# Waiting for POOL's own completion at every third indirect transfer in place of every second, in a two-layer graph network on one core

## The chip, the cores and the metric

The kernel runs on one core of a Trainium2 chip. The time is the device time of one execution in microseconds (us). TensorE is PE, VectorE is DVE, ScalarE is ACT, GpSimd is POOL, SyncE is SP.

## The reference

There are N = 100,000 nodes of 128 float32 features and E = 25,000 edges (`src`, `dst`), sorted by `dst`. Two layers follow each other, each with a residual and a layernorm over the features:

```python
x_col = x[col]                                   # row = src, col = dst
feat = concat([x_col, x[row] - x_col], -1)
messages = relu(feat @ W1 + b1) @ W2 + b2
out = segment_max(messages, col)                 # 0 where a node has no edge
x = layernorm(x + out)                           # layer 0

agg = segment_sum(x[src], dst)
h = relu((x + agg) @ W1 + b1) @ W2 + b2
x = layernorm(x + (x @ Wres + bres) + h)         # layer 1
```

Most nodes are the destination of no edge. For them both layers are dense work on their own row alone; rows that have edges must be computed with their neighbours and replace the dense result.

## The kernel before, in words

**Dense work.** Every row of x goes through as if it had no edges: 196 units of 512 rows, four units a body (`SLOTS`), 49 bodies. SP loads a unit and stores its result, DVE normalizes (`x <- x_in, rs_a` is the scaling of the first layernorm), PE transposes and multiplies, ACT evacuates.

**Edge work.** The edges are cut into `GROUPS` = 49 groups of `ROWS` = 512 edges, each group in `TILES` = 4 tiles of 128. One indirect transfer moves one tile: 128 rows of 128 float32, whose row numbers stand in a column of `idx`. All of them are issued by POOL, in an order written out by hand:

1. `gather_src(g)`: the src rows of group g from x into `edge_rows`, a buffer that holds all edges; 38 of the 49 groups first, with four groups of `gather_dst` after group 24.
2. `gather_dst(g)`: the dst rows into `xd_rows`, four slots of one group each. It waits until PE has transposed the group four before it (`tx_done`). After each fourth group one of the remaining 11 src groups is gathered.
3. After both tables of the first layer's edge results are stored (`tabled`) and all rows in `edge_rows` are scaled (`scaled_done`): the gathers of layer 1 from `x1e_table` into `edge_rows`, 49 groups.
4. The scatters of the 49 groups of results from `edge_rows` into the output. The scatter of group g waits for its result (`res_done`) and for the dense stores that cover its rows, so that it overwrites them; the number of stores is read from `stores_16` by POOL's sequencer (`stores_needed`, L635), for group g + 1 ahead of the last of group g's four scatters. At the end of the edge list that is all of the dense stores.

These are 4 x 196 = 784 indirect transfers, all through `gather` (L586) and `scatter` (L593).

**How the engines weave both.** `walk` gives each engine the same order: a body of dense work; then one dense unit a step beside the search for the place of each src row (`step_s`); then half a dense unit a step beside the edge work of layer 0 (`step_a`); then one dense unit a step beside that of layer 1 (`step_b`); then dense work alone. SP copies each gathered group of `edge_rows` into `xs_rows` (`copy_xs`, `copy_xz`, four slots), two groups ahead. In layer 0, DVE runs one scan a group for the segment maximum (L876); in layer 1 one for the sum (L923), and adds the dst rows (`xsT <- shared, x1eT`, L934).

**The pacing.** A transfer's `then_inc(done, 16)` counts when its data has landed. Apart from it, `pace` gives every second transfer a second semaphore, `s_issued`, that POOL itself raises when it has finished the instruction, and `issued_pair` lets POOL wait for it before it issues anything further. The data may still be under way then. All four kinds of transfer share one counter, and since a group has four tiles, the waits stand behind the second and the fourth tile of each group.

Of the kernel before, what the change touches and what calls it, by code (L numbers as in the profile page):

```python
# [44 lines left out]
def gnn_program(nc, x, src, dst, e_w1, e_b1, e_w2, e_b2, w1, b1, w2, b2, wres, bres, out):  # L45
# [21 lines left out]
    with ctx:  # L67
# [6 lines left out]
        def sem(name):  # L74
            return ctx.enter_context(nc.semaphore(name))
# [121 lines left out]
        s_issued = sem("descriptors_written")  # L197
# [357 lines left out]
        def _(pool):  # L555
# [12 lines left out]
            pool.wait_ge(s_dv, SRC_IDX_STEP)  # L568
            SRC, DST, SCAT, PLACE = range(4)
            issued = [0]  # L570

            def pace(kw):

                issued[0] += 1
                if issued[0] % 2 == 0:
                    kw["engine_sem"] = s_issued

            def issued_pair():
                if issued[0] % 2 == 0:
                    pool.wait_ge(s_issued, issued[0] // 2)  # L580

            def gather(to, table, what, t, done):
                kw = {}
                pace(kw)
                rows, err = (GROUPS * ROWS, False) if what == PLACE else (N, True)
                nc.gpsimd.indirect_dma_start(to, None, table, bass.IndirectOffsetOnAxis(idx[:, what, t:t + 1], 0),  # L586
                                             bounds_check=rows - 1, oob_is_err=err, **kw).then_inc(done, 16)
                issued_pair()

            def scatter(table, frm, t, done):  # L590
                kw = {}
                pace(kw)
                nc.gpsimd.indirect_dma_start(table, bass.IndirectOffsetOnAxis(idx[:, SCAT, t:t + 1], 0), frm, None,  # L593
                                             bounds_check=N - 1, oob_is_err=False, **kw).then_inc(done, 16)
                issued_pair()

            def gather_src(g):
                j, r = divmod(g, SLOTS)
                wait(pool, src_gathered[r], 16 * TILES * j)
                for t in range(TILES):  # L600
                    gather(edge_rows[:, cut(g * TILES + t)], x, SRC, g * TILES + t, src_gathered[r])

            def gather_dst(g):
                j, r = divmod(g, SLOTS)
                wait(pool, dst_gathered[r], 16 * TILES * j)
                wait(pool, tx_done, g - SLOTS + 1)
                for t in range(TILES):
                    gather(xd_rows[:, r, cut(t)], x, DST, g * TILES + t, dst_gathered[r])
# [19 lines left out]
            for g in range(GROUPS):  # L628
                j, r = divmod(g, SLOTS)
                wait(pool, z_gathered[r], 16 * TILES * j)  # L630
                for t in range(TILES):
                    gather(edge_rows[:, cut(g * TILES + t)], x1e_table, PLACE, g * TILES + t, z_gathered[r])
# [7 lines left out]
            for g in range(GROUPS):  # L640
                j, r = divmod(g, SLOTS)
                wait(pool, final[r], 16 * TILES * j)
                pool.wait_ge(res_done, g + 1)
                if g < WHOLE:
                    for k in range(SLOTS):
                        pool.wait_ge(stored[k], count)
                    pool.nop().then_inc(s_turn, 1)
                elif g == WHOLE:
                    for k in range(SLOTS):
                        pool.wait_ge(stored[k], 16 * BODIES)  # L650
                for t in range(TILES):
                    if t == TILES - 1 and g + 1 < WHOLE:
                        count = stores_needed(g + 1)
                    scatter(out, edge_rows[:, cut(g * TILES + t)], g * TILES + t, final[r])
# [817 lines left out]
```

## Time and profile before

| what | us |
|---|---|
| median of 3 runs | 1343.35 |
| lowest, highest | 1338.25, 1344.81 |
| profiled execution, its own time | 1332.02 |
| its span, first to last instruction | 1330.2 |
| mean granted clock of TensorE, share of full speed | 0.952 |

The span is what the profile shows; the profiled execution's own time is 1.8 us longer. It is one of the faster executions. Busy times are those of instructions on an engine; waits, branches and the handing over of DMAs are not counted. An "idle before" of a POOL transfer is the time from the end of the previous POOL instruction to its start, and behind the arrow stands who released it. "issue" means that nothing which the profile shows was waited for. Where the releaser of a POOL transfer is a "DMA" by the name of POOL's own transfers, the wait is the one for `s_issued`. Rows with the name POOLq are of POOL's sequencer, which hands instructions over to POOL's cores.

### The profile page before, as it was taken

How to read it: one execution, taken by the hardware profiler on the slowest of the kernel's cores; microseconds unless marked ns; L12 is line 12 of the kernel's file. 1: busy time of each engine (PE TensorE's matmuls, PEld its weight loads, DVE VectorE, ACT ScalarE, POOL GpSimd, SP SyncE). 2: the span in 40 equal slices, each digit the busy share in tenths (PEclk: the TensorE clock that was granted, in tenths of full speed). 3: DMA queues.
4: the chain of work that ended last, by engine and by line, in shares of the span. 5: the costliest groups of instructions: out<-in, count | busy, mean ns of one | idle time of the engine just before them, and what ended most of it. 6: DMA issues, size and time to landing. Idle time of an engine off the chain costs nothing. (4 is left out here: it accounts for less than half of the span.)

```text
span 1330.2 us, 32137 instructions
## 1 busy us (share of the span) xinstructions
PE 1123.7 (84%) x7512; PEld 853.2 (64%) x7512; DVE 1068.6 (80%) x5491; ACT 799.8 (60%) x2305; POOL 825.8 (62%) x797
## 2 busy tenths in 40 slices
PE   2699999998888878788759999999999999999500
PEld 1577777765555545455448888888887777777400
DVE  6599999989887887898838999999987888888400
ACT  0366666666665656667526666666666777777400
POOL 5666666656666666666256666666665666655654
PEclk9899999999998999999979999999999999999855
DMA  4477777756665667666436565656564556656310
GB/s 111 141 220 214 214 220 212 222 188 195 183 208 180 199 174 210 177 205 196 141 112 191 187 185 186 185 187 187 189 190 140 177 181 190 185 181 200 103 38 28
DMA packets 160366, 233.86 MB, mean 176 GB/s; under 512 B 26815, under 2 KB 69273, under 8 KB 160284
## 3 DMA queue, kind: packets, MB, share of 16 engines
q1 hardware_dynamic: 133612, 193.69, 46.7%
q0 software_dynamic: 25088, 38.81, 11.0%
q10 hardware_dynamic: 1584, 0.53, 0.2%
q14 instruction: 62, 0.51, 0.1%
q8 instruction: 20, 0.33, 0.1%
HBM read 129.48 MB, written 90.12 MB: 165 GB/s over the span
## 5 line engine op out<-in xcount | busy, mean ns | idle before, releaser
L1277 PE MATMUL psY<-wcr,xT 128*128 128x128 f32 x1568 | 305.0, 276 | 0.0
L1276 PE MATMUL psY<-wc,hT 128*128 128x128 f32 x1568 | 304.6, 276 | 0.0
L586 POOL DMA_INDIRECT edge_rows<-x1e_table,idx x196 | 210.8, 1075 | 133.2 <-DMA edge_rows<-x1e_table,idx 77.6
L593 POOL DMA_INDIRECT out<-edge_rows,idx x196 | 202.2, 1031 | 129.5 <-issue 76.4
L586 POOL DMA_INDIRECT edge_rows<-in_x,idx x196 | 206.9, 1056 | 116.0 <-DMA edge_rows<-in_x,idx 67.3
L586 POOL DMA_INDIRECT xd_rows<-in_x,idx x196 | 203.5, 1038 | 115.9 <-DMA xd_rows<-in_x,idx 67.3
L1276 PEld LDWEIGHTS psY<-wc,hT 128*128 128x128 f32 x1568 | 255.8, 193 | 15.0 <-issue 8.3
L1123 ACT ACTIVATE o_rows<-psY,rs_b 128x128 f32<-128x128 f32 x784 | 223.0, 367 | 66.7 <-DVE rs_b L741 66.5
L1277 PEld LDWEIGHTS psY<-wcr,xT 128*128 128x128 f32 x1568 | 239.9, 193 | 0.0
L1287 PE MATMUL psH<-xT,wc 128*128 128x512 f32 x392 | 204.5, 604 | 16.0 <-DVE deltas L787 10.6
L1103 ACT ACTIVATE sd_a<-mv_a,eps_col 128x4 f32<-128x4 f32 x196 | 58.3, 298 | 239.6 <-DVE mv_a L677 239.6
L672 DVE BATCH_NORM_STATS2 bn_b<-psY 128x6 f32<-128x128 f32 x784 | 174.4, 285 | 21.9 <-PE psY L1277 7.9
L691 DVE BATCH_NORM_STATS2 bn_a<-x_in 128x6 f32<-128x128 f32 x784 | 173.1, 271 | 0.3 <-DMA x_in<-in_x 0.3
L1267 PEld LDWEIGHTS psT<-ident,x 128*128 128x128 f32 x784 | 99.5, 143 | 106.2 <-issue 104.9
L1092 ACT ACTIVATE hT<-psH,bias_cols 128x512 f32<-128x512 f32 x196 | 131.0, 669 | 5.0 <-PE psH L1287 5.0
L682 DVE TENSOR_TENSOR x<-x_in,rs_a 128x512 f32<-128x512 f32 x196 | 130.6, 666 | 0.3 <-PE psT L1267 0.3
L1267 PE MATMUL psT<-ident,x 128*128 128x128 f32 x784 | 119.5, 276 | 0.9 <-DVE idx L1055 0.9
L1267 PE MATMUL psE<-ident,xs_rows 128*128 128x128 f32 x392 | 61.8, 281 | 60.8 <-ACT ehT L1161 51.6
L1100 ACT COPY xT<-psT 128x512 f32<-128x512 f32 x196 | 112.5, 574 | 0.5 <-PE psT L1267 0.5
L1267 PEld LDWEIGHTS psE<-ident,xs_rows 128*128 128x128 f32 x392 | 45.9, 143 | 98.2 <-issue 83.0
L923 DVE TENSOR_TENSOR_SCAN shared<-mask,shared,psE 128x512 f32<-128x512 bf16 x48 | 61.4, 1279 | 36.5 <-PE psE L1267 23.5
L1287 PEld LDWEIGHTS psH<-xT,wc 128*128 128x128 f32 x392 | 65.8, 194 | 35.6 <-issue 11.0
(135 smaller groups left out, 2042.6 us busy)
## 6 DMA issues: line engine op xcount, KB each, us to landing
x_in<-in_x SPq DMA_DIRECT2D x196, 256.0 KB
out<-o_rows SPq DMA_DIRECT2D x196, 256.0 KB
xs_rows<-edge_rows SPq DMA_DIRECT2D x98, 256.0 KB, 2.9
xs_rows<-src_dram SPq DMA_DIRECT2D x49, 256.0 KB, 4.3
mask<-mask_dram SPq DMA_DIRECT2D x98, 128.0 KB, 3.6
x1e_table<-shared SPq DMA_DIRECT2D x49, 256.0 KB, 2.8
x1eT_spill<-x1eT SPq DMA_DIRECT2D x49, 256.0 KB
x1eT<-x1eT_spill SPq DMA_DIRECT2D x49, 256.0 KB, 2.8
```

The lines of the kernel that those rows point to most:

```text
L586: nc.gpsimd.indirect_dma_start(to, None, table, bass.IndirectOffsetOnAxis(idx[:, what, t:t + 1], 0), bounds_check=rows - 1, oob_is_err=err ...
L593: nc.gpsimd.indirect_dma_start(table, bass.IndirectOffsetOnAxis(idx[:, SCAT, t:t + 1], 0), frm, None, bounds_check=N - 1, oob_is_err=False ...
L672: last = v.bn_stats(bn[:, t, :], rows[:, cut(t)])
L682: v.tensor_tensor(tiles(to), tiles(rows), rs.unsqueeze(2).broadcast_to([P, TILES, P]), ALU.mult).then_inc(done, 1)
L691: last = v.bn_stats(bn_a[:, k % 2, t, :], x_in[:, k, cut(t)])
L1092: a.activation(hT[:, k % 2, :], psH[:, :], ACT.Relu, bias=bias_cols[:, 2:3]).then_inc(hT_done, 1)
L1100: a.copy(xT[:, k, :], psT[:, :]).then_inc(xT_done, 1)
L1123: last = a.activation(o_rows[:, k, cut(t)], psY[k % 2][:, cut(t)], ACT.Copy, scale=rs_b[:, k, t:t + 1])
L1267: last = t_.transpose(to[:, cut(t)], rows[:, cut(t)], ident[:, :])
L1276: t_.matmul(to[:, cut(t)], h[:, cut(t)], wc2[:, :], start=False, stop=False, skip_group_check=True)
L1277: last = t_.matmul(to[:, cut(t)], xt[:, cut(t)], wcr[:, :], start=False, stop=t == TILES - 1, skip_group_check=True)
L1287: t_.matmul(psH[:, :], wc1[:, :], xT[:, k, :], start=True, stop=True).then_inc(w1_done, 1)
```

## The change

The counter of transfers stays, and a count of the waits is added. The semaphore is given to every third transfer (1, 2, **3**, 4, 5, **6**, ...) in place of every second one, and POOL waits behind it, in gathers and in scatters. The number of waits goes from 392 to 261. Nothing else differs: order, sizes and the other semaphores are the same. Since 3 does not divide the four tiles of a group, the waits now stand behind another tile in each group, in a pattern that repeats after three groups. For the scatters, whose first is transfer number 589, they stand behind the third tile in groups 0, 3, 6, ..., behind the second in groups 1, 4, ..., and behind the first and the fourth in groups 2, 5, ...

```diff
             issued = [0]
-
-            def pace(kw):
+            pauses = [0]
+            GATHERS_A_BURST, SCATTERS_A_BURST = 3, 3
+
+            def pace(kw, burst):
 
                 issued[0] += 1
-                if issued[0] % 2 == 0:
+                if issued[0] % burst == 0:
                     kw["engine_sem"] = s_issued
-
-            def issued_pair():
-                if issued[0] % 2 == 0:
-                    pool.wait_ge(s_issued, issued[0] // 2)
+                    pauses[0] += 1
+
+            def issued_burst(burst):
+                if issued[0] % burst == 0:
+                    pool.wait_ge(s_issued, pauses[0])
 
             def gather(to, table, what, t, done):
                 kw = {}
-                pace(kw)
+                pace(kw, GATHERS_A_BURST)
                 rows, err = (GROUPS * ROWS, False) if what == PLACE else (N, True)
                 nc.gpsimd.indirect_dma_start(to, None, table, bass.IndirectOffsetOnAxis(idx[:, what, t:t + 1], 0),
                                              bounds_check=rows - 1, oob_is_err=err, **kw).then_inc(done, 16)
-                issued_pair()
+                issued_burst(GATHERS_A_BURST)
 
             def scatter(table, frm, t, done):
                 kw = {}
-                pace(kw)
+                pace(kw, SCATTERS_A_BURST)
                 nc.gpsimd.indirect_dma_start(table, bass.IndirectOffsetOnAxis(idx[:, SCAT, t:t + 1], 0), frm, None,
                                              bounds_check=N - 1, oob_is_err=False, **kw).then_inc(done, 16)
-                issued_pair()
+                issued_burst(SCATTERS_A_BURST)
```

## Rows read from the trace of the kernel before

**Rows 1.** The page, POOL's busy time and the share of its DMA queue.
```profile
PE 1123.7 (84%) x7512; PEld 853.2 (64%) x7512; DVE 1068.6 (80%) x5491; ACT 799.8 (60%) x2305; POOL 825.8 (62%) x797
...
q0 software_dynamic: 25088, 38.81, 11.0%
```
**Rows 2.** Windows by stage: width, then busy us of each engine, granted clock, DMA share, GB/s.
```profile
60.00:281.00 221.00, 221.00 (x1928) 173.33 (x1927) 217.88 (x1142) 139.01 (x401) 143.31 (x137) 1.00 0.73 212
286.00:645.40 359.40, 296.98 (x1554) 195.48 (x1553) 302.85 (x1367) 229.67 (x603) 234.32 (x224) 0.98 0.64 191
668.20:989.40 321.20, 307.05 (x2098) 253.49 (x2097) 270.48 (x1356) 203.36 (x632) 210.74 (x196) 0.97 0.57 180
...
1251.30:1321.00 69.70, 0.00 (x0) 0.00 (x0) 0.18 (x1) 1.37 (x5) 43.15 (x44) 0.52 0.14 45
```
**Rows 3.** Waits of POOL: us in total, times, longest.
```profile
POOL edge_rows L586 <- issue: 65.0, 199, 2.1
```
**Rows 4.** Timeline of POOL, one pair's end and the next one's start: start, us, what, idle before.
```profile
205.42 1.01 POOL L586 DMA_INDIRECT edge_rows<-in_x,idx  x1 [0.30 <-issue]
207.24 1.01 POOL L586 DMA_INDIRECT edge_rows<-in_x,idx  x1 [0.81 <-DMA edge_rows<-in_x,idx]
```
**Rows 5.** The instructions of L586 and L293 on POOL's sequencer, 206.2 to 208.4 us.
```profile
L586 POOLq MOVE  x2: 29/29/29, 206.5 to 207.0; - x2
...
L293 POOLq EVENT_SEMAPHORE  x1: 17/17/17, 207.6 to 207.6; - x1
```
**Rows 6.** Timeline of POOL at its two real waits.
```profile
286.01 1.34 POOL L586 DMA_INDIRECT xd_rows<-in_x,idx  x1 [5.60 <-PE psE L1267]
...
644.37 1.01 POOL L586 DMA_INDIRECT xd_rows<-in_x,idx  x1 [0.30 <-issue]
668.18 1.00 POOL L586 DMA_INDIRECT edge_rows<-x1e_table,idx  x1 [22.80 <-DMA x1e_table<-shared]
```
**Rows 7.** Waits of PE, 300 to 640 us.
```profile
PE psE L1267 <- ACT ehT L1161: 47.5, 42, 2.0
```
**Rows 8.** Timeline of DVE, two scans of layer 0.
```profile
646.35 1.28 DVE L876 TENSOR_TENSOR_SCAN shared<-mask,shared,psE 128x512 f32<-128x512 bf16 x1 [0.43 <-PE psE L1381]
...
653.62 1.27 DVE L876 TENSOR_TENSOR_SCAN shared<-mask,shared,psE 128x512 f32<-128x512 bf16 x1
```
**Rows 9.** Timeline of DVE, its scalings of dense units.
```profile
752.46 0.66 DVE L682 TENSOR_TENSOR x<-x_in,rs_a 128x512 f32<-128x512 f32 x1
...
759.04 0.66 DVE L682 TENSOR_TENSOR x<-x_in,rs_a 128x512 f32<-128x512 f32 x1
...
1136.54 0.69 DVE L682 TENSOR_TENSOR x<-x_in,rs_a 128x512 f32<-128x512 f32 x1
...
1139.99 0.66 DVE L682 TENSOR_TENSOR x<-x_in,rs_a 128x512 f32<-128x512 f32 x1
```
**Rows 10.** Timeline of POOL: second gathers of two groups, first scatters of two groups.
```profile
752.60 1.38 POOL L586 DMA_INDIRECT edge_rows<-x1e_table,idx  x1 [0.30 <-issue]
...
759.20 1.37 POOL L586 DMA_INDIRECT edge_rows<-x1e_table,idx  x1 [0.30 <-issue]
...
1251.28 0.98 POOL L593 DMA_INDIRECT out<-edge_rows,idx  x1 [1.08 <-issue]
...
1257.71 0.98 POOL L593 DMA_INDIRECT out<-edge_rows,idx  x1 [1.08 <-issue]
```
**Rows 11.** The instructions of L635 and L593 on POOL's sequencer, 1267 to 1268 us.
```profile
L635 POOLq TENSOR_LOAD <-stores x1: 286/286/286, 1267.0 to 1267.0; - x1
...
L593 POOLq MOVE  x1: 29/29/29, 1267.5 to 1267.5; - x1
```
**Rows 12.** Timeline of SP, its last stores (start, and us until the last is handed over).
```profile
1238.82 14.45 SPq L385 DMA_DIRECT2D out<-o_rows  x6
```
**Rows 13.** All of L682's and L934's operations on those tiles: ns min/median/max, first to last start.
```profile
L682 DVE TENSOR_TENSOR x<-x_in,rs_a x196: 651/659/693, 10.0 to 1238.7; 128x512 f32<-128x512 f32 x196
...
L934 DVE TENSOR_TENSOR xsT<-shared,x1eT x49: 658/660/693, 680.1 to 1004.9; 128x512 f32<-128x512 f32 x49
```

## The prediction

> **What bounds the kernel now.** I read the page's first part, then the waits of POOL, then windows over the stages. The reader is to see that the busiest engine, PE, does not set the end: from 1251.3 us on PE has nothing left and DVE 0.18 us, while POOL alone works on for 70 us [rows 1, 2]. POOL is busy for only 62% of the span, yet most of its idle time is short and of its own making: 0.81 us from one transfer's end to the next's start after a transfer that POOL waited for, 0.30 us where it did not wait [rows 4]. A pair costs 1.01 + 0.30 + 1.01 + 0.81 = 3.13 us. POOL makes 784 such transfers in an unbroken chain, with two real waits for others: 5.60 us before the xd_rows gather at 286.01, and 22.80 us before the first gather from x1e_table at 668.18 [rows 6].
>
> These waits cut the run into pieces. Up to 281 us (dense work and the search for places) PE is busy in every microsecond [rows 2], and POOL waits at the end for the first edge step: so this is not POOL's stretch. From 286 to 645 POOL gathers xd_rows and late src rows, and never waits for a consumer. Nor does PE wait for POOL: its waits of 300 to 640 are for ACT alone, as in the one row that holds most of them [rows 7]. One edge step takes 7.3 us (DVE's scan at 646.35 and 653.62) [rows 8]; POOL needs on average 5 transfers for it, 7.8 us, and lives on its lead of four slots. It ends at 645.4 and DVE's scan of the last full step but one runs at 653.62, the transposes of the last group just before it [rows 6, 8]. So this stretch belongs to the engines, but POOL is only some 5 us ahead. From 668.2 to 989.4 POOL gathers 196 tiles, from 991.4 to 1321.0 it scatters 196. PE is busy in nearly all of the gathering stretch, but the gathers go into a buffer that holds all edges, so POOL needn't wait for PE and PE can't be what POOL's end hangs on. The end is: tables stored, 196 gathers, 196 scatters, plus the 9.2 us behind the last scatter (1330.2 - 1321.0).
>
> **A coupling.** In these two stretches about one transfer in four takes nearer 1.4 us than 0.99. At 752.60 a transfer starts while DVE's `x <- x_in, rs_a` runs from 752.46 to 753.12; it takes 1.38 [rows 9, 10]. The excess, 0.39, is what was left of the DVE operation, 0.52, less 0.13 us. So a start that falls in the first 0.54 us of such an operation is held to its end. This locks POOL to the engines: a group of four, of the natural length 4 x 0.99 + 2 x 0.30 + 2 x 0.81 = 6.18 us is stretched to DVE's 6.6 (752.46 and 759.04; POOL's second transfers at 752.60 and 759.20) [rows 9, 10]. Scatters: 4 x 0.98 + 2 x 0.30 + 0.81 + 1.08 = 6.41 natural, as after 1251 us (1251.28 to 1257.71), and about 6.9 beside DVE (two dense units of 3.45: 1136.54 and 1139.99) [rows 9, 10].
>
> **The change, part by part.** It drops 392 - 261 = 131 waits, and moves the rest to every third transfer, so they no longer stand at the group borders.
>
> *The pause.* Its price over a start without one is 0.81 - 0.30 = 0.51 us. The sequencer's rows explain it: after the wait, MOVE at 206.5, the next transfer's MOVE at 207.0 (so some 0.55 us to hand over one transfer), the first transfer's start at 207.24. At 207.6, with the first of the pair still running, the sequencer has handed over the second too and stands at a later instruction [rows 4, 5]. A third would be handed over by 208.2, before the first ends at 208.25. The trace never shows a third in a row. Lower bound of its idle time: 0.30, the second's. Upper: 0.81, what the wait costs, or in the worst case 2.10, the longest idle time that is put down to "issue" [rows 3]. I take 0.30, since the nearest row is a second transfer already waiting in the queue, and the third's handover is hidden in the same way. The Trainium skill (Advanced Engine Details and Errata, Engine Queue Depths) gives GpSimd a queue of 8, by which the third also fits and the sum stays; no row here shows the depth. Were a transfer to fill several places of it, the third would be the slow one of the second rival.
>
> *Up to 668 us.* 392 transfers lose 65 or 66 pauses, 33 us; 14 us of it before 286, where POOL then waits about 20 us in place of 5.6, and 19 us behind, where the wait for the tables grows from 22.8 to about 40. Cover: the edge chain of the engines. Gain of the end: 0. If that cover were gone (POOL slower than now by over 5 us in this stretch), every further microsecond would count.
>
> *Gathers, 668 on.* Three groups (12 transfers): 12 x 0.99 + 8 x 0.30 + 4 x 0.81 = 17.52 us. Holds by DVE: two operations (the other is `xsT <- shared, x1eT`) [rows 13], open for 0.54 us each in 6.6 us, mean hold 0.27: 12 x 1.08/6.6 x 0.27 = 0.5. So 18.0, times 49/3 = 294 us; now 321.2: gain 27. Without a hold 286 (gain 35), with as many as now (0.4 a group) 306 (gain 15). The first tiles come only 0.5 us earlier, so the entry of this stage hardly moves. The consumers: DVE and PE go on at 6.6; results stand ready for the scatters, which start at about 964 and need only those of their own group.
>
> *Scatters.* The read of `stores_16` (TENSOR_LOAD at 1267.0, the next MOVE at 1267.5) lies behind the third scatter, hidden now by a running transfer [rows 11]. In each third group it will stand behind a pause: 0.81 + 0.5 = 1.3. The border (1.08 now, every time) is behind a pause in one group of three. Three groups: 12 x 0.98 + 8 x 0.30 + (0.81 + 0.81 + 1.08 + 1.3) = 18.16, with holds 12 x 0.54/3.45 x 0.27 = 0.5 in five sixths of it 18.6, times 49/3 = 304 us; now 329.6: gain 25. Without holds 297 (gain 32), with today's (0.45 a group) about 317 (gain 12).
>
> *The sum.* 27 + 25 = 52 us; ends: 15 + 12 = 27, and 35 + 32 = 67. A floor cuts the upper one: the last group waits for all dense stores, the last of which is issued at about 1253 [rows 12]. With a 0.8 us start, four scatters in 5.3 us and the 9.2 us behind, and nothing for its landing, no span is under 1268: gain at most 62. The profiled execution has 1332.0 us around its span of 1330.2, so 1332.0 - 52 = 1280. It lies 11.3 us under the median of 1343.35; I take the same 52 off that: 1291. The likeliest case's own range is 1283 to 1316.
>
> *A rule against it.* DVE's operation was never longer than 0.693 us (least 0.651) in 196 times, with a POOL transfer running most of the time [rows 13]: denser starts don't slow DVE. The Trainium skill (SBUF — State Buffer, SBUF: two separate sides) says of the shared port pair that whoever starts first keeps it for the whole instruction; by that, DVE would be held for up to 1 us at a start and the dense work would stretch. The trace shows the hold in one direction only, so nothing is added for it.
>
> **Rivals.** (1) *The third start isn't free but costs near what was saved*, 0.45 to 0.7 us: for it, that nothing in the trace shows three in a row; against it, the sequencer's lead. Break-even: 52 / (2 x 65.3) = 0.40 us above 0.30, so 0.70; where the locking to DVE then fills up the slack, rather 0.55. Time: 1335 to 1350, take 1343.
>
> (2) *Slower: three in a row are one too many.* POOL's core, or the handover behind two waiting ones, makes the third start as late as behind a pause, or later. At 0.81: gathers 12 x 0.99 + 4 x 0.30 + 8 x 0.81 + 0.5 = 20.06, 328 us (+6); scatters 20.6, 338 us (+8); and before 645 a triple costs 4.95 against 4.70 now, 0.085 x 224 = 19 us more, of which 5 are covered: +14. Sum +28: 1371. At 1.08 some +80. It decides from 0.75 us on. For it speaks that POOL has idle times without a releaser of up to 2.1 us [rows 3]; against it, that 199 of them sum to 65.0 us, 0.33 each: nearly all are 0.30.
>
> (3) *Other work gives it back*: POOL's traffic, 11% of the DMA engines' time [rows 1], comes denser, and later loads stretch the dense work. DMA is busy 0.57 to 0.64 in the stretches that count [rows 2], and dense may end 60 us late before it decides. No change, 1340.
>
> **Chances.** Forecast 0.56; rival 1 0.14; rival 2 0.27; rival 3 0.03. Within 0.5% (6.7 us, about what a measurement can tell here) holds most of 1 and 3. Faster 0.58, same 0.13, slower 0.29. For 8 in 10 the range goes from 1281 (0.04 below) up to rival 2's first price, 1372 (0.15 above).
>
> **What the profile after would show.** Right: in bursts of three, idle 0.30, 0.30, 0.81; 261 idle times of 0.81 or more behind a completion; the wait before the first x1e_table gather near 40 us, still at about 668; gathers over by 958 to 964, scatters by 1262 to 1275, with 1.3 us of idle where the read of `stores_16` follows a pause; PE's last matmul still at 1249. Wrong: a third transfer with an idle time or duration of its own over 0.55 us; the first x1e_table gather later than 670; the holds by DVE growing until the group period is again 6.6 and 6.9.

## The result: 14% slower, and the profile after

| | median of the runs | lowest, highest |
|---|---|---|
| before, same chip | 1340.8 us | 1337.31, 1344.81 |
| after | 1534.41 us | 1521.22, 1548.95 |

The ratio is 1.141, with a 95% interval of 1.1304 to 1.1516. The forecast was 1291, its range 1281 to 1372. The profiled execution of after took 1548.95 us, its span is 1547.1; the traces are compared by their spans, 1330.2 and 1547.1. The ratio leaves out the slowest execution of after, which is the profiled one, so it differs a little from the quotient of the medians, and the traces lie 217 us apart where the medians lie 194 apart. Line numbers of after are 3 higher than before's.

First POOL itself. The timeline of POOL after, in the search stretch (columns as in [rows 4]):
```profile
75.95 1.01 POOL L589 DMA_INDIRECT edge_rows<-in_x,idx  x1 [0.30 <-issue]
77.77 1.01 POOL L589 DMA_INDIRECT edge_rows<-in_x,idx  x1 [0.81 <-DMA edge_rows<-in_x,idx]
79.08 1.01 POOL L589 DMA_INDIRECT edge_rows<-in_x,idx  x1 [0.30 <-issue]
80.40 1.01 POOL L589 DMA_INDIRECT edge_rows<-in_x,idx  x1 [0.30 <-issue]
82.23 1.01 POOL L589 DMA_INDIRECT edge_rows<-in_x,idx  x1 [0.81 <-DMA edge_rows<-in_x,idx]
```
This is the forecast to the hundredth: 0.30, 0.30, 0.81, and the third transfer as cheap as the second [rows 4]. In the scatters the read of `stores_16` behind a pause makes 1.37 us of idle time (1094.18), where 1.3 was forecast.

Now the other engines. The same windows as in [rows 2], and then a stretch in which POOL works and the one behind it, in which POOL waits:
```profile
60.00:281.00 221.00, 189.01 (x1354) 133.98 (x1353) 154.94 (x799) 98.56 (x278) 141.62 (x135) 0.92 0.55 161
286.00:645.40 359.40, 296.14 (x1689) 200.80 (x1688) 281.00 (x1320) 210.19 (x556) 176.99 (x172) 0.94 0.58 173
668.20:989.40 321.20, 232.92 (x1248) 171.18 (x1248) 190.87 (x905) 144.00 (x407) 187.21 (x183) 0.88 0.42 129
...
60.00:265.00 205.00, 173.90 (x1229) 122.73 (x1227) 140.68 (x724) 88.23 (x249) 141.01 (x135) 0.92 0.54 161
268.00:350.00 82.00, 81.89 (x721) 64.93 (x720) 80.84 (x432) 53.27 (x154) 0.00 (x0) 1.00 0.59 172
```
In 60 to 281 us PE runs 1354 matmuls where it ran 1928 [rows 2], and DVE and ACT fall with it: 799 for 1142, 278 for 401. The last two rows matter most. While POOL works, PE does 1229 / 205 = 6.0 matmuls per us; once POOL has nothing to do (x0) the same loop goes on at 721 / 82 = 8.8, the pace of before (1928 / 221 = 8.7), with the granted clock at 1.00. So nothing is wrong with PE's own work: it is held while POOL's transfers run.

What the hold looks like, in the timeline of PE after beside the burst of POOL above:
```profile
78.42 0.18 PE L1345 MATMUL psE<-place_w,shared 128*128 128x2 f16 x1
79.13 0.16 PE L1341 MATMUL psE<-place_w,match 128*128 128x2 f16 x1 [0.53 <-issue]
79.16 0.17 PE L1343 MATMUL psE<-place_w,shared 128*128 128x2 f16 x1
79.90 0.16 PE L1345 MATMUL psE<-place_w,shared 128*128 128x2 f16 x1 [0.57 <-issue]
79.92 0.16 PE L1341 MATMUL psE<-place_w,match 128*128 128x2 f16 x1
80.63 0.16 PE L1343 MATMUL psE<-place_w,shared 128*128 128x2 f16 x1 [0.54 <-issue]
```
Matmuls of 0.16 us, most of them with an idle time put down to "issue", come in twos, one two every 0.7 to 0.8 us, from 78.5 us on, in the middle of the burst, until about the time when its pause begins (81.41).

Where the 217 us of span came from, at POOL's landmarks. The timeline of POOL after:
```profile
351.26 1.01 POOL L589 DMA_INDIRECT xd_rows<-in_x,idx  x1 [85.66 <-PE psE L1270]
...
773.25 1.01 POOL L589 DMA_INDIRECT edge_rows<-x1e_table,idx  x1 [37.52 <-DMA x1e_table<-shared]
...
1069.90 1.02 POOL L596 DMA_INDIRECT out<-edge_rows,idx  x1 [1.99 <-issue]
...
1373.14 0.98 POOL L596 DMA_INDIRECT out<-edge_rows,idx  x1 [22.22 <-DMA out<-o_rows]
...
1537.00 0.98 POOL L596 DMA_INDIRECT out<-edge_rows,idx  x1 [0.81 <-DMA out<-edge_rows,idx]
```
- Search stretch: the first xd_rows gather of slot 4 comes at 351.26, not 286.01 [rows 6]: +65.
- Layer 0: the first x1e_table gather at 773.25, not 668.18: 105 late, so another +40.
- Gathers of layer 1: 773.2 to 1067.9, 294.7 us where they took 321.2: -26.5, the forecast's gain of 27, the only place where it is seen.
- Scatters: 1069.9 to 1538.0, 468 us for 330: +138. By the waits of POOL, 147.4 us in 15 waits are for the dense stores ("DMA out<-o_rows"): the dense work has fallen behind, and the scatters that overwrite its rows have to wait for it.

65 + 40 - 26.5 + 138 = 217.

### The profile page after: what moved, and what is told of

Its sections match the earlier page's. It is cut to its first block, busy times and chain, and to the rows that moved or that the text cites. A ratio compares the mean times of both kernels' runs of the same rounds, so it can differ in the third digit from the quotient of the medians.

```text
span 1547.1 us, 32074 instructions
## 1 busy us (share of the span) xinstructions
PE 1240.1 (80%) x7512; PEld 913.8 (59%) x7512; DVE 1072.1 (69%) x5491; ACT 809.8 (52%) x2305; POOL 809.0 (52%) x797
## 3 DMA queue, kind: packets, MB, share of 16 engines
q0 software_dynamic: 25088, 38.81, 9.4%
## 4 chain that ended last, share of the span: by engine, by line
PE 40%; DVE 19%; issue 17%; another core or an unknown queue 12%; ACT 7%; DMA 2%; SPq 1%; DVEq 1%; ACTq 0%; POOL 0%; POOLq 0%
PE psH L1290 7%; PE psY L1280 6%; PE psY L1279 6%; PE psE L1270 4%; PE psT L1270 3%; DVE bn_b L675 3%; DVE bn_a L694 3%; PE psY L1276 2%; DVE shared L926 2%; PE psE L1384 2%; PE psE L1280 2%; PE psE L1279 2%; ACT o_rows L1126 1%; PE psE L1328 1%
## 5 line engine op out<-in xcount | busy, mean ns | idle before, releaser
L596 POOL DMA_INDIRECT out<-edge_rows,idx x196 | 199.9, 1020 | 270.2 <-DMA out<-o_rows 147.4
L1279 PE MATMUL psY<-wc,hT 128*128 128x128 f32 x1568 | 310.9, 279 | 2.7 <-issue 2.0
L1280 PE MATMUL psY<-wcr,xT 128*128 128x128 f32 x1568 | 309.9, 279 | 3.2 <-issue 2.6
L1279 PEld LDWEIGHTS psY<-wc,hT 128*128 128x128 f32 x1568 | 260.5, 196 | 23.0 <-issue 14.5
L589 POOL DMA_INDIRECT edge_rows<-x1e_table,idx x196 | 199.9, 1020 | 132.2 <-issue 66.5
L1280 PEld LDWEIGHTS psY<-wcr,xT 128*128 128x128 f32 x1568 | 243.0, 195 | 6.7 <-issue 5.7
L1290 PE MATMUL psH<-xT,wc 128*128 128x512 f32 x392 | 225.5, 659 | 23.8 <-DVE deltas L790 8.5
L1270 PEld LDWEIGHTS psT<-ident,x 128*128 128x128 f32 x784 | 105.8, 150 | 124.2 <-issue 124.1
L1270 PE MATMUL psT<-ident,x 128*128 128x128 f32 x784 | 127.7, 286 | 6.1 <-issue 5.9
L1270 PE MATMUL psE<-ident,xs_rows 128*128 128x128 f32 x392 | 65.9, 292 | 74.1 <-ACT ehT L1164 47.7
L1290 PEld LDWEIGHTS psH<-xT,wc 128*128 128x128 f32 x392 | 71.4, 212 | 52.4 <-issue 26.4
```

Of the source, the lines that this page charges most:

```text
L1270: last = t_.transpose(to[:, cut(t)], rows[:, cut(t)], ident[:, :])
L1279: t_.matmul(to[:, cut(t)], h[:, cut(t)], wc2[:, :], start=False, stop=False, skip_group_check=True)
L1280: last = t_.matmul(to[:, cut(t)], xt[:, cut(t)], wcr[:, :], start=False, stop=t == TILES - 1, skip_group_check=True)
L1290: t_.matmul(psH[:, :], wc1[:, :], xT[:, k, :], start=True, stop=True).then_inc(w1_done, 1)
```

## The experiments

The same program took very different times on different chips, so each run is read against the kernel before on its own chip: 1361.46 on chip 11 (e1 to e4), 1335.95 on chip 13 (e5 to e8), 1338.56 and 1337.53 on chip 9 (e9 to e12; e17, e18), 1366.45 on chip 8 (e13 to e16). Chips are named by their numbers; the number of the chip on which the result above was taken is not on record.

### Which half, and what about three in a row (chip 11)

**e1, e2: threes in the gathers alone, in the scatters alone.**
```diff
-GATHERS_A_BURST, SCATTERS_A_BURST = 3, 3
+GATHERS_A_BURST, SCATTERS_A_BURST = 3, 2     # e1;  e2: 2, 3
```


> Bursts of three for the gathers only, pairs for the scatters. In the changed kernel PE's instructions came in a trickle (0.7 us apart) wherever POOL ran bursts of three, and at full rate where POOL waited for others. Theory A (two transfers handed over behind a running one hold up the other engines): everything up to the last gather as in the changed kernel (search over at about 350 in place of 281 us, last gather near 1068), then dense work at full rate, 1440 to 1490 us. Theory B (POOL's denser work as such, whatever its grouping): the same here. Theory C (the fault is in the scatters' part or in the dense stores alone): near 1340 us.

> Pairs for the gathers, bursts of three for the scatters only. Theories A and B: up to the last gather as before (989 us), scatters at 6.0 to 6.2 us a group in place of 6.9, but the dense work beside them slower by a quarter; POOL and the dense work end near each other, 1310 to 1350 us. Theory C: most of the 190 us loss is here, over 1450 us.

e1: 1552.06, ratio 1.137 (1.123 to 1.151). e2: 1430.73, ratio 1.048 (1.039 to 1.057). Both halves cost. e1 lies above all that was foreseen for it (1440 to 1490 by theory A), e2 between its two forecasts (1310 to 1350, over 1450). In e2, whose first 588 transfers are the pairs of before, the slot-4 gather came at 325.56 us behind a wait of 47.72, where the trace of before has 286.01 and 5.60: on this chip PE falls behind in the search stretch with pairs too.

**e3: no pause, but never more than one transfer handed over behind the running one; e4: bursts of four.**
```diff
-                if issued[0] % burst == 0:
-                    kw["engine_sem"] = s_issued
-                    pauses[0] += 1
+                kw["engine_sem"] = s_issued
...
-                if issued[0] % burst == 0:
-                    pool.wait_ge(s_issued, pauses[0])
+                if issued[0] > 1:
+                    pool.wait_ge(s_issued, issued[0] - 1)
...
-GATHERS_A_BURST, SCATTERS_A_BURST = 3, 3
+GATHERS_A_BURST, SCATTERS_A_BURST = 4, 4     # e4
```


> Every transfer raises the semaphore, and POOL waits after transfer n only for n - 1: never more than one is handed over behind the running one, and POOL still has no pause (0.30 us between transfers). Theory A (depth of the handover): the engines keep their pace (search over near 281 us, edge step of layer 1 6.6 us), POOL's transfers 1.3 us apart, the time falls to the dense work's floor, 1275 to 1295 us. Theory B (density of POOL's work): at least as slow as the changed kernel, 1530 us or more.

> Bursts of four, waits at the group borders only. Theory A: longer time with two or more waiting, so slower than bursts of three, 1580 to 1700 us. Theory B: rate only 0.04 us a transfer denser, so about 10% more of the same loss, 1540 to 1570 us. Theory D (it was the waits falling inside groups, against the waits for data at the borders): back near 1300 to 1340 us.

e3: 1825.9, ratio 1.339 (1.328 to 1.350). e4: 1737.78, ratio 1.273 (1.261 to 1.285). The windows of the search stretch, one fence for each of e2, e1, e4 and e3 (columns as in [rows 2]):
```profile
60.00:281.00 221.00, 198.88 (x1558) 145.51 (x1577) 179.90 (x924) 113.02 (x322) 140.93 (x136) 0.98 0.61 182
```
```profile
60.00:281.00 221.00, 178.31 (x1258) 125.63 (x1274) 148.23 (x758) 93.19 (x264) 143.47 (x135) 0.91 0.53 154
```
```profile
60.00:281.00 221.00, 148.66 (x798) 97.50 (x807) 94.95 (x487) 60.12 (x170) 140.46 (x135) 0.71 0.38 113
```
```profile
60.00:240.00 180.00, 28.01 (x78) 17.18 (x79) 11.27 (x62) 8.73 (x24) 130.59 (x130) 0.52 0.22 62
245.00:470.00 225.00, 220.54 (x1888) 173.79 (x1913) 217.45 (x1144) 139.09 (x400) 0.00 (x0) 0.98 0.58 169
```
Pairs 1558 matmuls, threes 1258, fours 798 in 221 us on one chip; without a pause 78 in 180 us, 0.43 per us, and 8.4 again as soon as POOL is idle. The granted clock falls with them (0.98, 0.91, 0.71, 0.52, the last near the lower level of 1.2 GHz): it follows PE's standing still and is back at 0.98 when POOL is idle, so it is no cause. e3 has no more transfers handed over ahead than pairs have, and PE stands all the same, so a third one in the queue is not what holds it; e4 puts the pauses back at the group borders and is slower than threes, so their place is not it either. On this chip the loss grows as POOL pauses less. Whether the length of a burst decides or the share of the pauses, these four don't separate. The timeline of PE in e3 shows how slow the stream becomes:
```profile
65.86 0.37 PE L1278 MATMUL psY<-wcr,xT 128*128 128x128 f32 x1 [2.87 <-issue]
68.66 0.37 PE L1277 MATMUL psY<-wc,hT 128*128 128x128 f32 x1 [2.43 <-issue]
71.45 0.37 PE L1277 MATMUL psY<-wc,hT 128*128 128x128 f32 x1 [2.43 <-issue]
74.25 0.37 PE L1278 MATMUL psY<-wcr,xT 128*128 128x128 f32 x1 [2.43 <-issue]
77.06 0.37 PE L1278 MATMUL psY<-wcr,xT 128*128 128x128 f32 x1 [2.43 <-issue]
```
One matmul every 2.80 us, with its weight load between (at 67.26, 70.06, ...), so one instruction every 1.40 us; POOL's transfers start every 1.32 us there, so it isn't one for one. Nor is it only PE's issuing that is late. The timelines of DVE and of ACT in e3:
```profile
100.33 0.89 DVE L673 BATCH_NORM_STATS2 bn_b<-psY 128x6 f32<-128x128 f32 x4 [44.90 <-remote]
```
```profile
117.14 0.59 ACT L1101 COPY xT<-psT 128x512 f32<-128x512 f32 x1 [9.83 <-remote]
```
The matmul at 77.06 is the last that fills this psY, and PE starts nothing more until 119.15. DVE begins on psY 23 us after it. ACT's copy waits in the program only for semaphores that PE raises, and begins 40 us after PE's last instruction and 9.83 us after ACT's own one before. So either what PE reports as done arrives late, or DVE's and ACT's own instructions are held as well; the trace doesn't tell which. POOL is not untouched: from 94.67 to 117.85 us its idle times grow from 0.30 to 0.39 and, four times, to between 1.2 and 1.8. So PE's low count here is in part the engines' waiting in turn for one another: PE starts nothing for 41.7 us from 77.4 on.

### More pause (chip 13)

**e5: a pause behind each transfer** (1, 1). **e6: threes, with a longer pause.**
```diff
                 if issued[0] % burst == 0:
                     pool.wait_ge(s_issued, pauses[0])
+                    rest.append(pool.value_load(row_number[0:1, 0:1], min_val=0, max_val=P))
```


> POOL's own completion waited for after every transfer. Theory 1 (PE gets its instructions and completions through only while POOL pauses; what counts is the share of pauses): 0.81 us of pause for 1.01 us of work, the other engines at full pace: 1739 or a few more PE matmuls in 60 to 260 us, the first xd_rows gather of slot 4 not later than POOL itself brings it. POOL becomes the bound: 784 x 1.82 = 1427 us from about 65 us on, plus 9 behind: near 1500, in layer 1 every transfer 1.82 apart. Theory 2 (the stall comes from the third transfer alone, pairs are entirely free): the same here, and no PE pace better than in the kernel before. Rival (the placement of pauses at group borders matters, not their share): no different from pairs, so also POOL-bound. What tells them apart is whether an engine step gets shorter than with pairs: 4.45 us a search step and 6.6 us a layer-1 step if pairs cost nothing.

> Bursts of three, but behind each wait the sequencer also reads one register from SBUF, which makes the pause some 1.35 us in place of 0.81: by share of pause (1.35 in 4.96 us, 0.27) it equals pairs (0.81 in 3.13, 0.26). Theory 1 (share or length of pause decides; PE's backlog drains in it): the engines' pace returns, the search stretch ends as before within some 15 us (first slot-4 xd_rows gather near 290 to 300), PE over 1650 matmuls in 60 to 260 us; time near POOL's own 784 x 1.65 us = 1294 us, bounded by it from layer 1 on: 1350 to 1400. Theory 2 (length of the burst decides: 3 us without a pause stalls PE, whatever follows): the search stretch stays at about 350 us, PE near 1200 matmuls, time 1540 or above.

e5: 1541.56, ratio 1.154 (1.152 to 1.157). e6: 1417.11, ratio 1.062 (1.060 to 1.065). In both PE runs at full pace in 60 to 281 us (1929 and 1931 matmuls): these two are slow because POOL is. In e6 the pauses measured 1.36 (1.35 was foreseen), a transfer costs (3 x 1.01 + 2 x 0.30 + 1.36) / 3 = 1.66 us against 1.565 for pairs, and the first x1e_table gather comes at 714.9 us in place of 672.0 (e7, the same chip). The times of e5 and e6 lie above what was foreseen (near 1500, 1350 to 1400). e6 also bears out a step of the prediction: in the layer-0 edge stretch POOL was said to be "only some 5 us ahead", and once it is 6% slower the stretch is POOL's. That threes need a longer pause is not shown by e6, since threes with the usual pause were never run in the search stretch on chip 13, and e8 below shows this chip to bear them in another stretch.

**e7: pairs, and no pause at all in the last 11 groups of scatters. e8: threes in the x1e_table gathers alone.**
```diff
+                tail[0] = g >= 38                      # e7, in the loop over the scatters
-                if issued[0] % burst == 0:
+                if issued[0] % burst == 0 and not tail[0]:
...
+            layer1[0] = True                           # e8, ahead of layer 1's gathers; False behind them
-                if issued[0] % burst == 0:
+                if issued[0] % (3 if layer1[0] else 2) == 0:
```


> Pairs as before up to the scatter group 37; from group 38 on (the last 11 groups, beyond about 1245 us, where no other engine works) no completion is waited for at all. Theory 1: with nobody to stall, POOL's saving is kept: 22 pauses x 0.51 = 11 us less, unless the dense stores' landing binds; 1330 against 1343, ratio 0.991 to 0.996. Theory 2: the same. Rival (the loss in the changed kernel has to do with POOL's own queue and not with other engines' work): no gain or a loss in this tail too, scatters there with an idle time over 0.30.

> Bursts of three in the 196 gathers from x1e_table alone, pairs before and behind. Theory 1: up to 668 us as before; the gathers then take 294 us in place of 321 (POOL's side as forecast), but the dense work and edge steps that run beside them are stretched, by 20 to 30% of 294 us; the scatters come to wait for dense stores, the end 40 to 80 us later: 1390 to 1420. Rival (the damage is done in the search stretch alone and carried on from there): the gathers end at 962, the scatters at about 1292, time 1316, ratio 0.98.

e7: 1320.9, ratio 0.9888 (0.9867 to 0.9909). e8: 1311.03, ratio 0.9818 (0.9800 to 0.9836), the fastest kernel of the study. Theory 1 failed on e8: it foresaw 1390 or more, and the rival's 1316 was near. The windows over 700 to 940 us of before and of e8:
```profile
700.00:940.00 240.00, 238.62 (x1664) 197.63 (x1664) 215.22 (x1084) 161.86 (x506) 156.90 (x146) 1.00 0.60 189
```
```profile
700.00:940.00 240.00, 239.72 (x1658) 198.52 (x1657) 215.78 (x1094) 162.70 (x507) 162.84 (x159) 0.99 0.61 188
```
159 transfers in threes for 146 in pairs, with 1658 matmuls for 1664: next to nothing lost. The gathers take 671.72 to 966.4, 294.7 us, the forecast's 294.

### Stretch by stretch (chips 9 and 8)

**e9: threes in layer 0 alone. e10: pairs in the search stretch (168 transfers), threes behind. e11: pairs in layer 0, threes in layer 1, no pause from scatter group 36 on. e12: e2 again.** All by switching the size of the burst at a point of POOL's order:
```diff
-                if issued[0] % burst == 0:
+                if issued[0] % size[0] == 0:
...
+            size[0] = 3                     # e10: ahead of late = SRC_FIRST; e11: ahead of the x1e_table gathers
             late = SRC_FIRST
```


> Bursts of three in the first 392 transfers (to the end of layer 0), pairs from the first x1e_table gather on. Theory 1 (bursts of three stall PE where PE's stream of small instructions is densest, in the search stretch): the search stretch is some 65 us longer, as in the changed kernel, the first x1e_table gather near 770; in layer 1 POOL's pairs let PE run at full pace again, 1650 or more matmuls in a stretch of 240 us there, gathers 321 us, scatters 330 us; time near 1440. Theory 2 (a stall, once begun, goes on by itself): layer 1 stays as slow as in the changed kernel, time 1500 or more. Rival (the search stretch costs nothing by itself): 1340.

> Pairs in the first 168 transfers (the search stretch), bursts of three in all others. Theory 1: the search stretch ends as before (first slot-4 xd_rows gather at 286), the layer-0 edge steps are the engines' (ends at 645), the wait at the first x1e_table gather grows from 23 to about 40 us, gathers 294 us, scatters 304 to 320 us; time 1285 to 1305, ratio 0.96 to 0.975: the blind forecast's own sum. Rival (three in a row cost the engines something in every stretch and layer 1 alone had room for it): the layer-0 edge steps or the scatter stretch are longer, with PE matmuls per microsecond below the kernel before; time 1320 to 1400.

> Pairs in layer 0, bursts of three in the gathers from x1e_table and in the scatters of groups 0 to 35, no completion waited for in the scatters of groups 36 to 48. Theory 1: gathers 294 us, scatters near 310 and a few us less in the tail; the floor of the dense stores (1268 us span) is near: time 1275 to 1295, ratio 0.955 to 0.97. Rival (the scatter stretch, with 1478 matmuls and 1213 DVE operations in 220 us, stalls under threes as the search stretch does): the scatters wait for dense stores, time 1330 or above.

> The kernel with pairs in the gathers and bursts of three in the scatters once more, on the chip of these other runs. In its first run its search stretch was 40 us longer than that of the kernel before though both have the same instructions there, on a chip on which the kernel before took 1361 us in place of 1336 to 1343. If that was the chip: the search stretch ends at 286 us here, and what is left is the scatters' own, 1310 to 1320 by theory 1. If it was something in the program (the place of its instructions in memory, say): again near 1430.

e9: 1441.03, 1.075 (1.069 to 1.082). e10: 1483.87, 1.106 (1.100 to 1.112). e11: 1476.1, 1.093 (1.083 to 1.103). e12: 1366.97, 1.015 (1.011 to 1.020), where it had 1430.73 on chip 11. e12 matches neither of its two expectations (1310 to 1320, near 1430): the slot-4 gather came at 295.36, 9 us later than in the trace of before. e9 came out as foreseen (near 1440): 1385 matmuls in 60 to 281 us, the first x1e_table gather at 773.30 behind a wait of 38.5 us, and later nearly the full pace (1541 matmuls in 800 to 1040 us, before 1647; 1123 in 1070 to 1240, before 1142). e10 and e11 did not: they had to show the gain of e8 and lost about 10%. e11 has e8's instructions up to the scatters; its window of layer 1:
```profile
700.00:940.00 240.00, 176.43 (x974) 138.06 (x973) 128.79 (x640) 97.44 (x298) 162.32 (x159) 0.86 0.38 118
```
974 matmuls where e8 ran 1658, with the same 159 transfers. Chip or program?

**e13: the changed kernel again; e14: e8 again; e15: e7 again; e16: threes in the search stretch alone** (e10's switch the other way round). All on chip 8.

> The changed kernel once more, beside the others on one chip. By the chip theory (each chip bears its own number of transfers in a row): about 1530 wherever the kernel before shows 1336 to 1343, 1550 where it shows 1360. It is the yardstick for the others here: PE matmuls in 60 to 260 and in 240 us of layer 1.

> Threes in the x1e_table gathers alone. If the chip decides: on a chip like 13 (kernel before 1336, pairs without a stall in the search stretch) 1311 again, and PE at some 1650 matmuls per 240 us of layer 1; on a chip like 9 or 11 (pairs with 1660 or fewer matmuls in 60 to 260 us) layer 1 stalls, under 1100 matmuls, time 1400 to 1450. If the program decides: 1311 in either case, ratio 0.98.

> Pairs, and no completion waited for in the last 11 groups of scatters. Nobody works beside that tail, so on any chip the 11 us of pauses are saved: ratio 0.988 to 0.993. Rival: on a chip where pairs stall a little the dense work is late and the tail not free of it, ratio 1.00 or above.

> Threes in the first 168 transfers alone. Theory 1: the search stretch is 65 to 80 us longer (about 1200 matmuls in 60 to 260 us), everything behind it runs as in the kernel before: 1400 to 1420. If a stall is carried on: 1450 or above, with layer 1 under 1500 matmuls in 240 us.

e13: 1652.81, 1.204 (1.192 to 1.217). e14: 1453.66, 1.064 (1.055 to 1.073). e15: 1380.15, 1.013 (1.003 to 1.023). e16: 1431.07, 1.046 (1.036 to 1.056). The e13 of 1652.81 is far above the 1550 foreseen for a chip where before shows 1360, so the time of the kernel before does not foretell how much threes cost. e14's window of layer 1:
```profile
700.00:940.00 240.00, 161.38 (x857) 128.59 (x869) 113.34 (x561) 85.04 (x253) 157.68 (x153) 0.81 0.35 109
```
The same program: 1658 matmuls on chip 13, 857 on chip 8. So the chip (or what goes on around it at that hour, which these runs can't separate) sets how dense POOL's transfers may come, and on chip 8 pairs already cost something: in e14 and e15, whose search stretch is that of before, there are 1634 and 1688 matmuls in 60 to 281 us, and 1926 in e7 and e8 on chip 13. e14's scatters waited 79.0 us for dense stores, at most 22.2 at once; e8's 15.8, at most 2.2. e16 says that a stall does not grow by itself behind its stretch: its slot-4 gather came 70 us later than e15's (379.53 and 309.97), and its end 65 us later than that of the kernel before, 51 later than e15's. e15 lost what e7 had won: the free tail is only free if the dense work is over by then, and in e15 its last group waited 14.28 us for dense stores.

### Bytes or POOL's writing (chip 9)

**e17: threes everywhere, but the gathers of layer 0 skip all rows but row 0. e18: its twin with the data.** e17 leaves out the gathered rows of layer 0, so their edges' results are not those of the reference.
```diff
+            nc.gpsimd.memset(xd_rows[:, :, :], 0.0)
+            nc.gpsimd.memset(edge_rows[:, :], 0.0).then_inc(s_issued, 1)
+            pool.wait_ge(s_issued, 1)
...
-                                             bounds_check=rows - 1, oob_is_err=err, **kw).then_inc(done, 16)
+                                             bounds_check=rows - 1 if what == PLACE else 0, oob_is_err=False, **kw).then_inc(done, 16)
```


> Bursts of three everywhere, but the 392 gathers of layer 0 skip every row but row 0 (their bound is 0), so that they move next to no data; edge_rows and xd_rows are filled with zeros by POOL first, which starts its transfers some 20 to 40 us later. If the bytes moved slow the other engines: PE at 8.7 matmuls per us in 80 to 260 us, as in the kernel before. If it is POOL's writing of transfers without a pause: PE at 4 to 6.5 per us there, as in its twin, though the traffic is gone. If skipped rows also shorten POOL's own 1.01 us, the pause share changes too and the test says less.

> The twin: bursts of three everywhere, the same two memsets ahead, all rows moved. PE at 4 to 6.5 matmuls per us in 80 to 260 us, time 1540 to 1660 by the chip.

e18: 1548.97, 1.155 (1.132 to 1.178). e17: 1710.55, 1.276 (1.256 to 1.295). The windows of e18, then of e17:
```profile
100.00:260.00 160.00, 138.66 (x995) 97.52 (x994) 115.53 (x593) 71.40 (x204) 110.20 (x105) 0.93 0.58 170
```
```profile
60.00:250.00 190.00, 28.76 (x87) 18.39 (x88) 12.66 (x65) 8.72 (x24) 145.53 (x147) 0.53 0.06 12
255.00:485.00 230.00, 221.02 (x1898) 172.61 (x1898) 213.91 (x1127) 138.28 (x398) 0.00 (x0) 0.97 0.54 162
```
With the DMA engines 6% busy PE runs 0.46 matmuls per us, against 6.2 in the twin, at 58%. Bytes don't do it. Packets are not ruled out: POOL's queue q0 has 25,088 of them in both runs. The expectation for e17 (4 to 6.5 per us) missed how far PE would fall. Why e17 is so much worse than its twin stands in its timeline of POOL:
```profile
159.55 0.99 POOL L592 DMA_INDIRECT edge_rows<-in_x,idx  x1 [0.30 <-issue]
160.85 1.00 POOL L592 DMA_INDIRECT edge_rows<-in_x,idx  x1 [0.30 <-issue]
162.15 1.00 POOL L592 DMA_INDIRECT edge_rows<-in_x,idx  x1 [0.30 <-issue]
163.45 1.00 POOL L592 DMA_INDIRECT xd_rows<-in_x,idx  x1 [0.30 <-issue]
```
Every idle time is 0.30: though the program waits at each third transfer, the wait costs nothing here, and the pause is gone (why the completion comes early is open). So e17 is e3 without data, and PE's pace is e3's: 0.46 and 0.43. The two have a transfer of 1.0 us every 1.3 in common, and a pace of PE nearly twenty times too low. The Trainium skill (Perfetto Trace Analysis, DMA Instruction — SWDGE (GPSIMD)) says that the record of such a transfer ends when POOL's cores have written the last descriptor, not when data has moved; the trace agrees: q0 moved 13.44 MB in e17 and 38.81 in e18, and most records are 0.99 to 1.01 us in both.

The two runs show something else by the way. The timeline of DVE in e17, while POOL fills edge_rows with zeros from 10.36 to 31.36 us:
```profile
14.91 16.54 DVE L1026 TENSOR_SCALAR brow<-brow,bsum 128x128 f32<-128x128 f32 x1
```
The same operation took 0.36 us before (at 15.06), and 16.53 in e18. It ends 0.1 us behind POOL's memset: here POOL held DVE, which its transfers did not do to the scalings of [rows 13].

## Why the prediction was wrong, step by step

**What held.** The price of a pause (0.51), the third start (0.30, taken from the second), the 1.3 us at the `stores_16` read, the 294 us of layer 1's gathers. Rivals 1 and 2, with 0.41 of the chance between them, were about the third start, and didn't occur. e8 is the forecast's sum for the gathers alone: 25 us gained by the medians (1335.95 - 1311.03), where the gathers' term said 27. e7 gained 15 from 22 pauses, where 22 x 0.51 = 11 (where the other 4 came from is open).

**The step that failed** is the cover: "Up to 668 us ... Cover: the edge chain of the engines. Gain of the end: 0", and with it "DVE and PE go on at 6.6" in the gathers. Both took the other engines' work as a thing of fixed length that POOL can only be ahead of or behind. The pause was booked as POOL's loss alone; the runs show that it was also what let PE's instructions through. It cost 65 us up to 286, 40 up to the tables, and 138 in the scatters. In the terms of the sum: the layer-1 gathers were entered at 773 in place of 668, their own 294 us came true, and the scatters took 468 us where the sum had 304. The prediction's own sign of being wrong, a first x1e_table gather later than 670, came true.

**The evidence used for it** was the paragraph "A rule against it": DVE's `x <- x_in, rs_a` at 0.651 to 0.693 us in 196 times [rows 13], hence "denser starts don't slow DVE". The row after is the same:
```profile
L685 DVE TENSOR_TENSOR x<-x_in,rs_a x196: 650/659/692, 10.1 to 1515.3; 128x512 f32<-128x512 f32 x196
```
True, and beside the point: the durations didn't change, the rate of issue did, and PE's, which was not looked at. The lock that the Trainium skill describes (SBUF — State Buffer, SBUF: two separate sides) would have lengthened this row, if POOL's transfers took it; the trace shows that it did not. That POOL can hold DVE with another instruction is what the 16.54 us in e17 show, so "in one direction only" is true of the transfers beside these scalings and not of POOL.

**The third rival** ("other work gives it back", 0.03, 1340 us) had the right direction and the wrong cause: DMA traffic. e17 took the traffic away and the stall grew; by the windows the share of the DMA engines fell from 0.73 to 0.55 in the search stretch after the change, since less was asked of them. Its size had no bound in the trace of before: PE was busy in all of 221 us, and no row showed it held. All that could be noted was that before never had more than two transfers in a row without a pause, 2.3 us (1.01 + 0.30 + 1.01), so that nothing was known of the other engines beyond.

**What is shown of the cause, and what isn't.** Shown: PE is held while POOL starts indirect transfers with few pauses, the more so the fewer the pauses (e2, e1, e4, e3 on one chip), and goes back to 8.3 to 8.8 matmuls per us within 3 to 5 us of POOL's stopping. It is not the bytes (e17), a third transfer in the queue (e3) or the place of the pause (e4). On each chip that ran both in the search stretch, threes cost much more than pairs. PE's matmuls from 60 to 281 us:

| chip | pairs | threes |
|---|---|---|
| 11 | 1558 (e2) | 1258 (e1) |
| 9 | 1835, 1851, 1834 (e10, e11, e12) | 1385 (e9) |
| 8 | 1634, 1688 (e14, e15) | 993, 1091 (e13, e16) |
| 13 | 1926, 1926 (e7, e8) | not run |

The traces of chips 11 and 8 lack about 1% of the matmuls (1558 for 1577 weight loads), far less than these differences. Shown too: how much a chip bears differs, from 1311 to 1454 us for one program. Open: the path that the engines share. That PE's instructions come slowly and that DVE and ACT begin late on what PE has finished (e3) speaks for something that every instruction must send or get; the packets of POOL's queue are a rival that no run removed. Loading of the program is an unlikely one: its queues moved 62 and 20 packets in before, after and e3 alike, for over 15,000 instructions of PE. The Trainium skill (NOTIFIC — the notification-queue block, Overflow: three behaviours, one of which stalls the engine) says that the block which writes such records always holds back within its own pipeline rather than lose a record there; by that, the stall could be a cost of being recorded. No run here can show it, since every timed execution lists spans and clocks, so all were recorded. Also open are why threes cost e8 nothing on chip 13 (no run of the changed kernel is on record for that chip), whether the length of a burst or the share of the pauses decides, and whether the pairs' loss on chips 8, 9 and 11 is the chip's alone, as no trace of the kernel before is on record as taken on them.

## What to carry to other kernels

Before a pause on POOL is booked as pure loss, ask what the other engines get done in it: compare the other engines' rate (instructions per us) in a window where POOL runs its transfers with one where it is idle, and watch the rate, not the durations. Removing pauses looks safe only where no other engine has work that matters (e7's tail on chip 13), and a gain near such an edge must be tried on more than one chip: e7 and e8 won 1 to 2% on one and lost 1 and 6% on another. No version here beats the kernel before on both.

## What the runs showed of the hardware

- PE's rate beside an unbroken run of 128-row indirect transfers on POOL (1.0 us each, every 1.3 us) was 0.43 to 0.46 matmuls per us, at times with one instruction every 1.40 us, against 8.7 before and 8.4 and 8.3 once POOL had stopped (e3, e17). DVE began 23 us, and ACT 40 us, after PE's last instruction on tiles that PE had finished (e3).
- One program took 1311 us on chip 13 and 1454 on chip 8, where the kernel before took 1336 and 1366.
- Where gathers skip nearly all their rows, the wait for POOL's completion left no pause: idle 0.30 at each start (e17), and PE was held as without any wait.
- Four transfers in a row follow each other with 0.30 us of idle time as well (e4), so the handing over was not the limit.
- A DVE TENSOR_SCALAR of 0.36 us took 16.5 while POOL ran a memset of 21 us, and ended with it (e17, e18); DVE's scalings beside POOL's transfers stayed at 0.65 to 0.69 us (before, after).
